# Self-attention stage: VectorE normalises the rows of the tile after next behind the second decay addition, and not at the beginning of the body

## The chip, the core and the metric

The kernel runs on one core of a Trainium2 chip. A core has five engines, each with an instruction queue of its own that is worked off in order: TensorE (PE in the profile, its weight loads PEld), VectorE (DVE), ScalarE (ACT), GpSimd (POOL) and SyncE (SP, which issues DMAs here). Engines meet only at semaphores: an instruction may wait until a semaphore has reached a value, and may raise one when it ends. An instruction that waits holds up everything behind it in its engine's queue. The metric is the device time of one launch in microseconds (us).

## What is computed

A layer with three parts, each adding to `x` (128 batches, 32 rows, width 128): a cross-attention over 257 context rows, a causal self-attention with a decay over the distance of rows, and a mixture of 8 experts. The change lies in the second part alone. Cut to what matters, that part is:

```python
Q, K, V = (proj(Wq, bq), proj(Wk, bk), proj(Wv, bv))        # of _layernorm(x); 16 heads of 8
scores = jnp.einsum('bhnd,bhmd->bhnm', Q, K) / jnp.sqrt(jnp.float32(dk))
scores = scores + power_law_mask(N, DECAY_SCALE)[None, None] # -0.25*log(lag), -inf above the diagonal
attn = jax.nn.softmax(scores, axis=-1)
out = jnp.einsum('bhnm,bhmd->bhnd', attn, V)
return out.transpose(0, 2, 1, 3).reshape(B, N, D) @ Wo + bo
```

## The kernel before

The three parts run one after the other, each in a block that all engines enter and leave together. The self-attention is the function `attend` (line 728 on). It works on 16 tiles of 8 batches. `X` holds the rows of all tiles in the core's memory, so this stage moves no data of its own from or to the chip's main memory.

The order of the work is written out by hand: every engine runs a function `body(t)` for t = 0 to 17, and each body has work of several tiles, so that the tiles run as a pipeline. What one tile goes through:

- VectorE takes statistics of the rows (`norm_stats`, `norm_mean`, `norm_var`, L791 to L803), GpSimd raises the variance to the power -1/2 (`power`, L910), and VectorE writes the normalised rows `xn` in two instructions (`norm`, L811).
- TensorE transposes `xn` (`turn`, L1005), ScalarE copies the result (`turned`, L941), TensorE projects it to queries and keys (`project`, L1011 and L1012), ScalarE spreads these (`projected`, L950 and L955).
- TensorE computes the scores in two halves of 4 batches (`scores`, L1033). For each half VectorE adds the decay (`add_decay`, L821), takes maxima (`maxima`, L826) and subtracts them (`less_maxima`, L831); ScalarE takes the exponential (L968); VectorE sums and inverts (L837, L842); GpSimd multiplies (`normalise`, L903, which writes `En`).
- TensorE transposes the probabilities (`turn_probs`, L1043), ScalarE copies them (`probs`, L975), TensorE multiplies them with the values (`weigh`, L1054), VectorE keeps each head's own part (`own`, L849), TensorE projects the output (`project_out`, L1064), GpSimd adds the output's bias to the rows (`bias`, L917), and VectorE adds the two (`add`, L857).

In body t the queues of the four engines hold, in this order:

- VectorE: `norm(t+2)`, then `add_decay(t,0)`, `maxima(t,0)`, `add_decay(t,1)`, `less_maxima(t,0)`, `maxima(t,1)`, `norm_stats(t+3)`, `less_maxima(t,1)`, `add(t-2)`, `norm_mean(t+3)`, the sums and inverses of both halves with `norm_var(t+3)` between, and `own(t-1)` for both halves.
- TensorE: `project(t+1)`, `scores(t,0)`, `scores(t,1)`, `turn_probs(t-1)` for both halves, `turn(t+2)`, `project_out(t-2)`, `values(t)`, `weigh(t-1)` for both halves.
- ScalarE: `projected(t+1)`, `probs(t-1,0)`, the exponential of half 0, `probs(t-1,1)`, the exponential of half 1, `turned(t+2)`, `values(t)`.
- GpSimd: `bias(t-2)`, `normalise(t,0)`, `power(t+3)`, `normalise(t,1)`.

So TensorE's `turn(t+2)` waits in body t for VectorE's `norm(t+2)` of the same body (L1001), and VectorE's `add_decay(t,h)` waits for TensorE's `scores(t,h)` (L817). `norm(t+2)` itself waits for `power(t+2)`, which GpSimd ran one body earlier, and for `turn(t+1)`, by which `xn` is free again.

Of the kernel before, what the change touches and what calls it, by code (L numbers as in the profile page):

```python
# [26 lines left out]
T = B // TB  # L27
# [700 lines left out]
def attend(nc, X, ident, hh_scaled, consts):  # L728


    with ExitStack() as s2:
# [42 lines left out]
        def tile_of(t):  # L774
            return X[:, t, :] if isinstance(t, int) else X[:, bass.ds(t, 1), :].rearrange("p a c -> p (a c)")

        def run(body):

            for t in range(T + 2):
                body(t)  # L780

        def later(t):
            return not (isinstance(t, int) and t == 0)

        with nc.Block() as block:
            @block.vector
            def _(dve):
                def norm_stats(t):
                    xt = tile_of(t)
                    for e in range(2):  # L790
                        i = dve.bn_stats(stat[:, e, :], xt[:, e * D:(e + 1) * D])  # L791
                    i.then_inc(n_stat, 1)

                def norm_mean(t):
                    dve.wait_ge(n_stat, t + 1)
                    dve.nop(nofuse=True)
                    for e in range(2):
                        i = dve.bn_aggr(mv[:, e, :], stat[:, e, :])
                    i.then_inc(n_mv, 1)

                def norm_var(t):
                    dve.wait_ge(n_mv, t + 1)
                    dve.tensor_scalar(var[:, :], mv[:, :, 1], EPS_LN, None, ALU.add).then_inc(n_var, 1)  # L803

                def norm(t):
                    dve.wait_ge(n_rs, t + 1)
                    if later(t):
                        dve.wait_ge(xt_ps, t)
                    xt = tile_of(t)
                    for e in range(2):  # L810
                        i = dve.tensor_scalar(xn[:, e, :], xt[:, e * D:(e + 1) * D], mv[:, e, 0:1], rs[:, e:e + 1],  # L811
                                              ALU.subtract, ALU.mult)
                    i.then_inc(n_xn, 1)

                def add_decay(t, h):
                    m = 2 * t + h
                    dve.wait_ge(s_ps, m + 1)  # L817
                    if later(t):
                        dve.wait_ge(en_sb, m - 1)
                    flat = E[:, h, :, :].rearrange("p u s -> p (u s)")  # L820
                    dve.tensor_tensor(flat, PS[h][:, :], decay[:, :, :].rearrange("p u s -> p (u s)"), ALU.add).then_inc(s_sb, 1)  # L821

                def maxima(t, h):
                    m = 2 * t + h
                    dve.wait_ge(s_sb, m + 1)
                    dve.tensor_reduce(mx[:, h, :], E[:, h, :, :], AX.X, ALU.max).then_inc(m_sb, 1)  # L826

                def less_maxima(t, h):
                    m = 2 * t + h
                    dve.wait_ge(m_sb, m + 1)  # L830
                    dve.tensor_tensor(E[:, h, :, :], E[:, h, :, :], mx[:, h, :].unsqueeze(2).to_broadcast([P, HB * NQ, L]),  # L831
                                      ALU.subtract).then_inc(d_sb, 1)

                def sums(t, h):
                    m = 2 * t + h
                    dve.wait_ge(e_sb, m + 1)
                    dve.tensor_reduce(sm[:, h, :], E[:, h, :, :], AX.X, ALU.add).then_inc(sum_sb, 1)  # L837

                def invert(t, h):
                    m = 2 * t + h  # L840
                    dve.wait_ge(sum_sb, m + 1)
                    dve.reciprocal(sm[:, h, :], sm[:, h, :]).then_inc(inv_sb, 1)  # L842

                def own(t, h):
                    m = 2 * t + h
                    dve.wait_ge(o_ps, m + 1)
                    if later(t):
                        dve.wait_ge(y_ps, t)
                    dve.tensor_tensor(Oc[:, :, HB * h:HB * h + HB, :].rearrange("p a b g -> p b a g"),  # L849
                                      PE_[h][:, :, :].rearrange("p j (a g) -> p j a g", g=NQ),  # L850
                                      hh_wide[:, :, :].rearrange("p q a -> p (q a)").unsqueeze(1).unsqueeze(3).to_broadcast(
                                          [P, HB, HQ * TB, NQ]), ALU.mult).then_inc(o_sb, 1)

                def add(t):
                    dve.wait_ge(y_ps, t + 1)
                    dve.wait_ge(xb, t + 1)
                    dve.tensor_tensor(tile_of(t), PY[:, :], Xb[:, :], ALU.add).then_inc(x2, 1)  # L857

                def body(t):
                    if t + 2 < T:  # L860
                        norm(t + 2)
                    if t < T:
                        add_decay(t, 0)
                        maxima(t, 0)
                        add_decay(t, 1)
                        less_maxima(t, 0)
                        maxima(t, 1)
                        if t + 3 < T:
                            norm_stats(t + 3)
                        less_maxima(t, 1)  # L870
                    if t >= 2:
                        add(t - 2)
                    if t + 3 < T:
                        norm_mean(t + 3)
                    if t < T:
                        sums(t, 0)
                        if t + 3 < T:
                            norm_var(t + 3)
                        invert(t, 0)
                        sums(t, 1)  # L880
                        invert(t, 1)
                    if 1 <= t <= T:
                        own(t - 1, 0)
                        own(t - 1, 1)

                for t in range(2):
                    norm_stats(t)
                    norm_mean(t)
                    norm_var(t)
                    norm(t)  # L890
                norm_stats(2)
                norm_mean(2)
                norm_var(2)
                run(body)

            @block.gpsimd
# [749 lines left out]
```

## Time and profile before

| | |
|---|---|
| median of 3 runs | 933.85 us (933.37 to 934.37) |
| the profiled execution | 933.31 us, of which its span (first to last instruction) is 931.4 us |
| span of the self-attention stage | about 459 to 620 us |
| busy in the span | PE 86%, DVE 87%, ACT 68%, POOL 44% |

Times in the trace are microseconds from the start of the span. A row of the timeline is a run of equal instructions: its start, the time from its first start to its last end, the engine, the line of the kernel, the operation, output<-inputs, the count, and in square brackets how long the engine sat idle before it and what released it. Instructions of one engine overlap a little, so what one costs in a busy queue is the time from its start to the next start.

### The profile page before, as it was taken

The page shows a single profiled execution, that of the slowest core. Times are in us where ns is not written, and L with a number is a line of the kernel's source. Part 1 is how long each engine was busy: PE and PEld are TensorE (multiplying, and loading weights), DVE is VectorE, ACT ScalarE, POOL GpSimd, SP SyncE. Part 2 cuts the span into 40 slices and gives each one's busy share as a digit, 9 for nine tenths or more (in the row PEclk, how much of TensorE's full clock was granted, in tenths as well). Part 3 has the DMA queues.
Part 4 walks back from the last instruction along what each step waited for, and adds up shares of the span by engine and source line. Part 5 has one row for each costly group of instructions (what it writes and reads, how often), then busy time and mean ns, then how long its engine had stood idle before and what let it go on. Part 6 is the DMA issues. An engine that isn't in the chain of part 4 may idle for free. (4 is left out here: it accounts for less than half of the span.)

```text
span 931.4 us, 32721 instructions
## 1 busy us (share of the span) xinstructions
PE 804.2 (86%) x10989; PEld 636.6 (68%) x10989; DVE 808.1 (87%) x2344; ACT 636.4 (68%) x2022; POOL 408.8 (44%) x420
## 2 busy tenths in 40 slices
PE   4898998899889889988669999979989898899882
PEld 2566666566666656665468888968878787788782
DVE  4888988988898889888659999957999999999994
ACT  3777777777777777777367777725767767776774
POOL 4222222322222222322114334344787777878785
PEclk9999999999999999999969999999999999999997
DMA  3221111111111111114000000000000000000000
GB/s 89 70 84 40 51 37 51 37 48 44 40 51 37 51 37 51 40 41 164 7 2 2 3 2 3 4 1 1 8 6 6 11 6 6 6 11 6 6 10 14
DMA packets 32717, 27.60 MB, mean 30 GB/s; under 512 B 3548, under 2 KB 32408, under 8 KB 32664
## 3 DMA queue, kind: packets, MB, share of 16 engines
q1 hardware_dynamic: 32664, 26.87, 9.8%
q8 instruction: 36, 0.59, 0.3%
q14 instruction: 17, 0.14, 0.1%
HBM read 24.76 MB, written 2.10 MB: 29 GB/s over the span
## 5 line engine op out<-in xcount | busy, mean ns | idle before, releaser
L544 ACT ACTIVATE E<-SC,neg_max 128x257 f32<-128x257 f32 x512 | 235.9, 474 | 101.8 <-DVE neg_max L604 101.8
L604 DVE TENSOR_REDUCE neg_max<-SC 128x1 f32<-128x257 f32 x512 | 181.9, 417 | 36.7 <-PE SC L401 34.1
L414 PE MATMUL ETP<-ident,E 128*128 128x128 f32 x1024 | 162.3, 286 | 37.9 <-ACT E L544 37.4
L613 DVE TENSOR_TENSOR Et<-ETP,mask_T 128x512 f32<-128x512 f32 x256 | 172.5, 684 | 15.5 <-PE ETP L414 14.4
L414 PEld LDWEIGHTS ETP<-ident,E 128*128 128x128 f32 x1024 | 108.8, 142 | 88.5 <-issue 78.4
L1311 PE MATMUL PO<-W,hid 128*128 128x128 f32 x1024 | 137.9, 278 | 18.7 <-ACT hid L1352 18.7
L1376 ACT ACTIVATE Y<-Z,zb,zs 128x128 f32<-128x128 f32 x256 | 111.0, 485 | 60.1 <-DVE zb L1531 60.1
L1311 PEld LDWEIGHTS PO<-W,hid 128*128 128x128 f32 x1024 | 131.2, 192 | 28.9 <-issue 21.5
L1300 PE MATMUL PH<-xT,W 128*128 128x256 f32 x512 | 135.4, 387 | 0.5 <-ACT xT L1344 0.5
L1352 ACT ACTIVATE hid<-PH,b1c 128x256 f32<-128x256 f32 x256 | 105.5, 463 | 19.3 <-PE PH L1300 17.8
L544 ACT ACTIVATION_READ_ACCUMULATOR E<-SC,neg_max 128x1 f32 x512 | 103.8, 203 | 0.0
L332 POOL TENSOR_TENSOR Qbd<-Qt,hh_scaled 128x512 f32<-128x512 f32 x32 | 40.7, 1272 | 131.1 <-ACT Qt L532 131.1
L401 PE MATMUL SC<-Kt,Qbd 32*128 32x257 f32 x1024 | 93.2, 433 | 2.1 <-DVE out_bias L709 0.6
L1300 PEld LDWEIGHTS PH<-xT,W 128*128 128x128 f32 x512 | 87.8, 192 | 9.7 <-ACT xT L1344 0.7
L433 PE MATMUL AV<-Et,V 128*32 128x128 f32 x2048 | 83.3, 279 | 0.1
L1202 POOL TENSOR_TENSOR XB<-xn,b2r 128x512 f32<-128x512 f32 x64 | 81.4, 1275 | 0.8 <-DVE xn L1427 0.8
L1208 POOL TENSOR_TENSOR zr<-zv,neg_half 128x8 f32<-128x8 f32 x32 | 60.0, 1875 | 39.6 <-DVE zv L1517 39.6
L1541 DVE TENSOR_TENSOR U<-Y,gr 128x512 f32<-128x512 f32 x64 | 71.2, 1112 | 5.4 <-POOL acc L1214 2.9
L903 POOL TENSOR_TENSOR En<-E,sm 128x512 f32<-128x512 f32 x32 | 33.4, 1048 | 95.4 <-DVE sm L842 95.4
L433 PEld LDWEIGHTS AV<-Et,V 128*32 128x32 f32 x2048 | 49.8, 109 | 32.6 <-DVE Et L613 26.3
L307 POOL TENSOR_TENSOR xrs<-xvar,neg_half 128x1 f32<-128x1 f32 x32 | 17.6, 550 | 119.3 <-DVE xvar L591 119.3
L525 ACT ACTIVATE Kt<-MISC 128x256 f32<-128x256 f32 x128 | 49.2, 384 | 25.5 <-PE MISC L382 17.4
(161 smaller groups left out, 1406.3 us busy)
## 6 DMA issues: line engine op xcount, KB each, us to landing
V<-in_ctx_dram SPq DMA_DIRECT2D x64, 256.0 KB, 2.6
xh<-in_x_dram SPq DMA_DIRECT2D x32, 64.0 KB, 2.2
last_rep<-in_ctx_dram SPq DMA_DIRECT2D x128, 2.0 KB
X<-in_x_dram SPq DMA_DIRECT2D x32, 64.0 KB
out_dram<-Xo SPq DMA_DIRECT2D x64, 32.0 KB, 1.5
W<-in_L_ffn_w_dram SPq DMA_DIRECT2D x1, 1024.0 KB
W<-in_L_ffn_w_dram SPq DMA_DIRECT2D x2, 512.0 KB
b2r<-in_L_ffn_b_dram SPq DMA_DIRECT2D x1, 512.0 KB
```

The source lines that it names most:

```text
L401: i = pe.matmul(SC[:, g, 0:S], Qbd[r, j // HB, j % HB, :, :].rearrange("p q l -> p (q l)"), Kt[r, j, :], start=True, stop=True)
L414: i = pe.transpose(ETP[s][:, c:c + P], E[:, j // HB, NQ * (j % HB) + 2 * s + u, k * P:(k + 1) * P], ident[:, :])
L433: i = pe.matmul(AV[32 * g:32 * g + 32, j % HB, :], V[:, j, k, 32 * g:32 * g + 32], Et[:, 2 * (j % 2) + g // 2, g % 2, k, :], start=(j % HB ...
L544: i = act.activation(E[:, h, at, :], SC[:, u, 0:S], ACT.Exp, bias=neg_max[:, j % 2, u:u + 1], accum_out=den[:, h, at:at + 1])
L604: dve.tensor_reduce(neg_max[:, j % 2, u:u + 1], SC[:, u, 0:S], AX.X, ALU.max, negate=True).then_inc(max_sb, 1)
L613: dve.tensor_tensor(Et[:, 2 * (j % 2) + s, :, :, :].rearrange("p u k c -> p (u k c)"), ETP[s][:, :], mask_T[:, :, :, :].rearrange("p u k c ...
L1202: pool.tensor_tensor(XB[:, 2 * p:2 * p + 2, :, :], xn[:, :, :].unsqueeze(1).to_broadcast([P, 2, 2, D]), b2r[:, 2 * p:2 * p + 2, :].unsquee ...
L1300: i = pe.matmul(PH[x % 2][:, a, :], W1[:, x, a * P:(a + 1) * P], xT[:, :], start=True, stop=True)
L1311: i = pe.matmul(PO[p % 2][:, 2 * (x % 2) + e, :], hid[:, x % 2, a, e * P:(e + 1) * P], W2[:, x, a, :], start=(a == 0), stop=(a == FH - 1))
L1352: i = act.activation(hid[:, x % 2, a, :], PH[x % 2][:, a, :], ACT.Gelu, bias=b1c[:, FH * x + a:FH * x + a + 1])
L1376: i = act.activation(Y[:, p % 2, k, :], Z[:, p, k, :], ACT.Identity, scale=zs[:, p // 2, f:f + 1], bias=zb[:, p // 2, f:f + 1])
L1541: dve.tensor_tensor(U[:, k, :, :].rearrange("p (x e) d -> p x e d", x=2), Y[:, k, :, :].rearrange("p (x e) d -> p x e d", x=2), gr[:, 2 * ...
```

## The change

In VectorE's `body(t)` the call of `norm(t + 2)` moves from the first place to the place behind `add_decay(t, 1)`. The functions that are called stay as they are, and so do the queues of the other engines.

```diff
                 def body(t):
-                    if t + 2 < T:
-                        norm(t + 2)
                     if t < T:
                         add_decay(t, 0)
                         maxima(t, 0)
                         add_decay(t, 1)
+                    if t + 2 < T:
+                        norm(t + 2)
+                    if t < T:
                         less_maxima(t, 0)
                         maxima(t, 1)
                         if t + 3 < T:
```

VectorE's queue where one body ends and the next begins, bodies 2 and 3, before (xn is the tile of normalised rows, PS the scores in the matmul output memory, E the scores with decay, Oc the heads' outputs; the names in brackets are the semaphores that an instruction waits for):

```order
L849 TENSOR_TENSOR Oc<-PE,hh_wide 128x4x32x4 [waits y_ps,o_ps2] x2
L811 TENSOR_SCALAR xn<-X,mv,rs 128x128 [waits xt_ps,n_rs]
L811 TENSOR_SCALAR xn<-X,mv,rs 128x128
L821 TENSOR_TENSOR E<-PS,decay 128x512 [waits en_sb,s_ps]
L826 TENSOR_REDUCE mx<-E 128x16 [waits s_sb]
L821 TENSOR_TENSOR E<-PS,decay 128x512 [waits en_sb,s_ps]
L831 TENSOR_TENSOR E<-E,mx 128x512 [waits m_sb]
```

and the same place now:

```order
L849 TENSOR_TENSOR Oc<-PE,hh_wide 128x4x32x4 [waits y_ps,o_ps2] x2
L821 TENSOR_TENSOR E<-PS,decay 128x512 [waits en_sb,s_ps]
L826 TENSOR_REDUCE mx<-E 128x16 [waits s_sb]
L821 TENSOR_TENSOR E<-PS,decay 128x512 [waits en_sb,s_ps]
L811 TENSOR_SCALAR xn<-X,mv,rs 128x128 [waits xt_ps,n_rs]
L811 TENSOR_SCALAR xn<-X,mv,rs 128x128
L831 TENSOR_TENSOR E<-E,mx 128x512 [waits m_sb]
```

The two instructions of `norm` stand behind two instructions that wait for the scores (`s_ps`); before, they stood ahead of them.

VectorE's queue at the end of the prologue and in body 0, before:

```order
L803 TENSOR_SCALAR var<-mv 128x2 [waits n_mv]
L811 TENSOR_SCALAR xn<-X,mv,rs 128x128 [waits xt_ps,n_rs]
L811 TENSOR_SCALAR xn<-X,mv,rs 128x128
L821 TENSOR_TENSOR E<-PS,decay 128x512 [waits s_ps]
L826 TENSOR_REDUCE mx<-E 128x16 [waits s_sb]
L821 TENSOR_TENSOR E<-PS,decay 128x512 [waits s_ps]
L831 TENSOR_TENSOR E<-E,mx 128x512 [waits m_sb]
```

and now:

```order
L803 TENSOR_SCALAR var<-mv 128x2 [waits n_mv]
L821 TENSOR_TENSOR E<-PS,decay 128x512 [waits s_ps]
L826 TENSOR_REDUCE mx<-E 128x16 [waits s_sb]
L821 TENSOR_TENSOR E<-PS,decay 128x512 [waits s_ps]
L811 TENSOR_SCALAR xn<-X,mv,rs 128x128 [waits xt_ps,n_rs]
L811 TENSOR_SCALAR xn<-X,mv,rs 128x128
L831 TENSOR_TENSOR E<-E,mx 128x512 [waits m_sb]
```

Here the normalisation of tile 2 leaves the prologue, in which VectorE waits for the first scores, and stands between instructions of body 0.

## Rows read from the trace of the kernel before

**Rows 1.** The page: busy time, share of the span, instructions of each engine.

```profile
PE 804.2 (86%) x10989; PEld 636.6 (68%) x10989; DVE 808.1 (87%) x2344; ACT 636.4 (68%) x2022; POOL 408.8 (44%) x420
```

**Rows 2.** Timeline of VectorE, one steady body (start, duration, engine, line, operation).

```profile
535.41 1.68 DVE L811 TENSOR_SCALAR xn<-X,mv,rs 128x128 f32<-128x128 f32 x2
537.01 0.68 DVE L821 TENSOR_TENSOR E<-PS,decay 128x512 f32<-128x512 f32 x1
537.73 0.69 DVE L826 TENSOR_REDUCE mx<-E 128x16 f32<-128x512 f32 x1
538.33 0.68 DVE L821 TENSOR_TENSOR E<-PS,decay 128x512 f32<-128x512 f32 x1
538.93 0.68 DVE L831 TENSOR_TENSOR E<-E,mx 128x512 f32<-128x512 f32 x1
...
544.43 1.68 DVE L811 TENSOR_SCALAR xn<-X,mv,rs 128x128 f32<-128x128 f32 x2
```

**Rows 3.** Timeline of GpSimd beside it.

```profile
535.28 1.05 POOL L903 TENSOR_TENSOR En<-E,sm 128x512 f32<-128x512 f32 x1
536.28 0.73 POOL L917 TENSOR_TENSOR Xb<-X,out_bias 128x256 f32<-128x256 f32 x1
```

**Rows 4.** Timeline of VectorE in the prologue.

```profile
461.31 0.60 DVE L811 TENSOR_SCALAR xn<-X,mv,rs 128x128 f32<-128x128 f32 x2 [0.82 <-POOL rs L910]
461.83 0.48 DVE L791 BATCH_NORM_STATS2 stat<-X 128x6 f32<-128x128 f32 x2
```

**Rows 5.** Timeline of TensorE, the same steady body.

```profile
533.22 0.70 PE L1011 MATMUL PA<-xT,Wq 128*128 128x256 f32 x2 [0.29 <-ACT xT L941]
...
534.19 1.95 PE L1033 MATMUL PS<-Kbd,Qbd 128*128 128x128 f32 x16
535.97 1.07 PE L1043 MATMUL PE<-ident,En 128*128 128x128 f32 x8
537.15 0.44 PE L1005 MATMUL PA<-ident,xn 128*128 128x128 f32 x2
537.42 1.95 PE L1064 MATMUL PY<-Wo,Oc 128*128 128x128 f32 x16
539.30 0.76 PE L1020 MATMUL PV<-Wv,xT 128*32 128x32 f32 x64
540.00 1.95 PE L1054 MATMUL PE<-Et,Vt 32*32 32x128 f32 x64
```

**Rows 6.** Timeline of TensorE, first half of the scores of the next body.

```profile
543.21 1.05 PE L1033 MATMUL PS<-Kbd,Qbd 128*128 128x128 f32 x8
```

**Rows 7.** Timeline of TensorE in the last bodies.

```profile
591.26 0.44 PE L1005 MATMUL PA<-ident,xn 128*128 128x128 f32 x2
...
597.06 1.95 PE L1033 MATMUL PS<-Kbd,Qbd 128*128 128x128 f32 x16
...
602.29 1.95 PE L1054 MATMUL PE<-Et,Vt 32*32 32x128 f32 x64
604.17 2.05 PE L1033 MATMUL PS<-Kbd,Qbd 128*128 128x128 f32 x16
```

**Rows 8.** Timeline of TensorE in bodies 1 and 2.

```profile
479.03 1.22 PE L1011 MATMUL PA<-xT,Wq 128*128 128x256 f32 x2 [3.18 <-ACT xT L941]
...
488.47 0.70 PE L1011 MATMUL PA<-xT,Wq 128*128 128x256 f32 x2
...
492.09 0.40 PE L1005 MATMUL PA<-ident,xn 128*128 128x128 f32 x2
```

**Rows 9.** Timeline of VectorE in body 1.

```profile
484.55 0.69 DVE L821 TENSOR_TENSOR E<-PS,decay 128x512 f32<-128x512 f32 x1 [0.30 <-PE PS L1033]
...
486.74 0.67 DVE L831 TENSOR_TENSOR E<-E,mx 128x512 f32<-128x512 f32 x1
```

**Rows 10.** Windows: length, busy us per engine, then PEclk, DMA share, GB/s.

```profile
476.00:479.00 3.00, 0.00 (x0) 0.00 (x0) 3.00 (x11) 1.73 (x5) 0.07 (x1) 0.86 0.02 5
488.00:590.00 102.00, 97.87 (x1954) 88.53 (x1943) 101.03 (x228) 74.84 (x173) 39.84 (x47) 1.00 0.01 3
611.00:619.00 8.00, 6.57 (x117) 5.70 (x107) 3.25 (x7) 1.20 (x2) 3.05 (x4) 1.00 0.01 2
```

## The prediction

> **What bounds the kernel now.** I read the page first: over the whole span no engine stands out, PE and DVE are at 86% and 87% [rows 1]. That is a mean over three stages, so next come the windows of the stage that the change touches. In the 102 us of its steady bodies VectorE is busy 101.03 us, TensorE 97.87 us [rows 10]: VectorE has no gap left and sets the pace. The timeline gives the pace: `norm` starts at 535.41 and again at 544.43, a body every 9.02 us [rows 2].
>
> Then I ask what each instruction of that full queue costs, and one is odd. The two instructions of `norm` hold VectorE from 535.41 to 537.01, 1.60 us [rows 2]. In the prologue the same two hold it from 461.31 to 461.83, 0.52 us, and end 0.60 us after they start [rows 4]. What differs is GpSimd: in the steady body `En` runs from 535.28 to 536.33 and `Xb` from 536.28 to 537.01 [rows 3], so `norm` runs beside GpSimd from end to end; its last instruction ends at 537.09, 0.08 us behind `Xb`. In the prologue GpSimd is idle meanwhile. So about 1.08 us of each body is time that `norm` loses beside GpSimd.
>
> The last view is TensorE's. It is almost as full, and in its queue `turn` stands in the middle: it starts at 537.15, 0.06 us behind the end of `norm`, while `turn_probs` ahead of it ended at 535.97 + 1.07 = 537.04 [rows 5]. So TensorE waits for `norm` even now, by some 0.1 us of empty array, and behind `turn` stand the longest pieces of the body. This wait decides the change.
>
> **The change part by part.** It adds and removes no instruction and no DMA. It moves two VectorE instructions past three others, in 14 bodies.
>
> *What VectorE saves.* GpSimd's `En` and `Xb` follow VectorE's inverses of the same body, and end 1.60 us behind the last `own` (535.41 to 537.01 [rows 2, 3]). In the new place `norm` comes 1.92 us behind `own` (add 0.72, maxima 0.60, add 0.60 [rows 2]), and later still by any wait for the scores. It then runs with GpSimd idle. I take 0.52 us of queue as in the prologue; the bounds are 0.52 and 1.60. VectorE's own work falls from 9.02 to 7.94 us a body. Were VectorE alone the limit, that would be 1.08 us a body.
>
> *What TensorE loses.* `norm(t+2)` now waits behind both halves of `scores(t)`, and TensorE's `turn(t+2)` of the same body waits for it. Behind `turn` in the queue stand `project_out`, `values` and `weigh`, then the next body's `project` and `scores`, and for those the next `add_decay` waits. That closes a ring through both engines which did not exist before: scores, add, maxima, add, norm, turn, and on to the next scores. Its length, piece by piece:
>
> - `turn` to `project_out` 0.27, to `values` 1.88, to `weigh` 0.70 [rows 5]. `weigh` to what follows: 1.88 where the next matmuls are ready (602.29 to 604.17 [rows 7]). Together 4.73.
> - `project` to `scores`: 534.19 - 533.22 = 0.97 [rows 5]. The 0.29 us that `project` waits for ScalarE now falls away, since ScalarE's copy hangs on the second `less_maxima`: from that to `project` it takes 1.73 (486.74 to 488.47 [rows 8, 9]), and in the ring more than 3 us lie between them.
> - First half of the scores to `add_decay(t,0)`: 1.05 for its matmuls [rows 6] and 0.05 for the crossing to VectorE, an estimate from the 0.06 of norm to turn above. 1.10.
> - `add_decay` 0.72, `maxima` 0.60, the second `add_decay` 0.60 [rows 2]. The second half of the scores (1.95 from the start of the 16 matmuls [rows 5]) is there in time: the second addition starts 1.10 + 1.32 = 2.42 behind that start.
> - `norm` 0.60 to its end [rows 4], 0.06 to `turn`.
>
> Sum: 4.73 + 0.97 + 1.10 + 1.92 + 0.60 + 0.06 = 9.38 us. VectorE's 7.94 lies inside and gains idle time instead of pace. The body goes from 9.02 to 9.38 us, 0.36 longer. On TensorE the same is seen as a pause: from the start of the scores to `turn` 3.68 us (before 537.15 - 534.19 = 2.96), of which scores and `turn_probs` fill 1.78 + 1.07, so 0.83 us stays empty. The bounds: with `weigh` at its whole duration, 1.95, the body takes 9.45; if matmuls, crossing and `norm` each overlap the next by a few hundredths more than I let them, 9.25. I take 9.38, made of start-to-start times throughout.
>
> *The start.* In body 0 `norm(2)` leaves a time in which VectorE was idle and enters its busy chain: `less_maxima` and all behind it, the exponentials and ScalarE's copy for `project(2)`, come 0.52 later, so `project(2)` moves from 479.03 [rows 8] to 479.55, and with it the scores and the second addition of body 1, from 484.55 [rows 9] to 485.07. `less_maxima(1,1)` follows 2.19 + 0.52 later (486.74 - 484.55 = 2.19 [rows 9]) at 487.78, 1.04 late; `project(3)`, which hangs on it, moves from 488.47 to 489.51. From there to `turn(4)` it is 0.97 + 3.68 = 4.65, so 494.16 against 492.09 [rows 8]: 2.07 late.
>
> *The steady part.* From `turn(4)` to `turn(15)` before: 591.26 - 492.09 = 99.17 in 11 bodies [rows 7, 8], 9.02 each. Now 11 x 9.38 = 103.18, 4.0 more.
>
> *The end.* From `turn(15)` to the scores of body 14 it was 597.06 - 591.26 = 5.80 [rows 7], now 4.73 + 0.97 = 5.70: 0.1 back. Bodies 14 to 17 have no `norm`, and TensorE runs through them without pause at first, so nothing else is given back. The expert stage begins after all engines have met and is unchanged.
>
> Sum: 2.07 + 4.0 - 0.1 = 6.0 us. On the profiled execution's own time, 933.31 (span 931.4 and 1.9 around it), that is 939.3; on the median of the runs, 0.54 higher, it is 939.85. I forecast 939.5.
>
> *The clock.* A longer pause in every body could cost TensorE its clock. In 476 to 479 it had no matmul and its granted clock fell (mean 0.86); the project of 479.03 took 1.22 us against 0.70 at full clock [rows 5, 8, 10]. In 611 to 619 it stood empty for 1.43 of 8 us, a larger share than 0.83 of 9.38, and kept 1.00, the level of 2.4 GHz [rows 10]. So I put the clock at no cost. The Trainium skill, "TensorE: Matmul & The Clock Gate", section "A second HAM failure mode: psum-queue depth-cycling", speaks against this: it tells of a kernel in which small pauses between groups of matmuls in every iteration made the clock swing and cost throughput. By that rule the change would end as the fourth rival below; the steady bodies of before, with their small pauses at 1.00, do not show it.
>
> **The rivals.**
>
> *1. Faster: VectorE was the limit, and its 1.08 us come through.* The place is `add_decay(t,0)`, which can start earlier once `norm` is gone from ahead of it; it decides if the stretch from scores to `turn` comes in under 2.96 + 0.36 = 3.32 us, so that the ring is no longer than 9.02. The floor is then TensorE's own work, 97.87 / 102 x 9.02 = 8.65 us a body [rows 10]; 12 bodies at 0.37 less, 4.4 us, give 929.5. For it speaks VectorE's full queue. Against it: three VectorE instructions of 0.60 or more and `norm` itself lie one behind the other in that stretch, and none of them can start before the scores.
>
> *2. No change.* The saved VectorE time and TensorE's wait pay for one another: the ring is some 0.3 shorter than the sum of its pieces and the start costs less, because more of it lies beside waits for the first scores. Then the body stays at 9.0 and the time at 933 to 935.5. Against it: every piece is a start-to-start time already, with the overlap in it.
>
> *3. It does not do what it says: `norm` meets GpSimd in the new place too.* Then the ring is 1.08 longer, 10.46 us, and 12 bodies add 13 us: 952. Against it: `Xb` ended 1.60 us behind `own`, and the new `norm` starts behind `own` by 1.92 us of other instructions and by VectorE's new idle time, 9.38 - 7.94 = 1.44, or 3.36 in all.
>
> *4. The clock falls in the pause.* At 1.22 against 0.70 us for the same matmuls the 6.8 us of TensorE in the ring become some 11.8, 5 us more in each body that it strikes; in every fifth body 11 us more, 950.
>
> **How the numbers follow.** Two runs of this kernel differ by up to 1 us, so under 0.2% (1.9 us) is no change. Forecast 0.76, rival 1 0.07, rival 2 0.09, rival 3 0.03, rival 4 0.05. Slower: forecast and rivals 3 and 4, 0.84; same 0.09; faster 0.07. The forecast's own range: body 9.25 to 9.45 (2.5 to 4.7 us), start 1 to 2.5, so 3.5 to 7 us more, 936.8 to 940.9. The range of 8 in 10 reaches down into the no-change case, 935, and up by the unknown price of `norm` behind a busy queue, 942.
>
> **What would show it.** Right: `norm` at some 0.6 us for its two instructions in the steady bodies; VectorE idle before `add_decay(t,0)` for about 1.2 us, released by TensorE's scores; TensorE's `turn` waiting for `xn` for about 0.8 us in each of 12 bodies; the wait of `project` for ScalarE gone; a body of 9.38 us, VectorE under 90% busy in it. Wrong: a body under 9.02 us, with `turn` free of waits (rival 1); `norm` still above 1.2 us (rival 3); a granted clock under 1.00 between 490 and 600 (rival 4).

## The result and the profile after

The changed kernel is slower: 940.8 us median (939.32 to 940.96) against 933.93 (933.37 to 934.37), four runs each, ratio 1.007, 95% interval 1.0053 to 1.0088. A second set of runs of the same two kernels, on one chip, gave 939.95 against 932.24, ratio 1.007 (1.0049 to 1.0091). The forecast was 939.5, its range 935 to 942. The profiled execution has a span of 937.4 us, 6.0 more than before.

The page after, busy time and share of the span, against [rows 1]:

```profile
PE 801.3 (85%) x10989; PEld 634.8 (68%) x10989; DVE 796.9 (85%) x2344; ACT 637.3 (68%) x2022; POOL 409.3 (44%) x420
```

VectorE works 11.2 us less than before and the kernel takes longer: the work saved has turned into waiting. Where it waits, the timeline of VectorE in a steady body shows, against [rows 2] (start, duration, what ran, in brackets the idle time ahead and what ended it):

```profile
535.82 1.22 DVE L849 TENSOR_TENSOR Oc<-PE,hh_wide 128x512 f32<-128x512 f32 x2
538.16 0.69 DVE L821 TENSOR_TENSOR E<-PS,decay 128x512 f32<-128x512 f32 x1 [1.12 <-PE PS L1034]
538.89 0.69 DVE L826 TENSOR_REDUCE mx<-E 128x16 f32<-128x512 f32 x1
539.49 0.68 DVE L821 TENSOR_TENSOR E<-PS,decay 128x512 f32<-128x512 f32 x1
540.09 0.60 DVE L811 TENSOR_SCALAR xn<-X,mv,rs 128x128 f32<-128x128 f32 x2
...
547.53 0.69 DVE L821 TENSOR_TENSOR E<-PS,decay 128x512 f32<-128x512 f32 x1 [1.12 <-PE PS L1034]
```

`norm` takes 0.60 us for its two instructions and not 1.68. In exchange VectorE stands idle for 1.12 us ahead of the first decay addition, until TensorE has the scores. The body takes 547.53 - 538.16 = 9.37 us; before it was 9.02.

The timeline of TensorE in the same body, against [rows 5]:

```profile
536.10 0.70 PE L1012 MATMUL PA<-xT,Wq 128*128 128x256 f32 x2
...
537.07 1.95 PE L1034 MATMUL PS<-Kbd,Qbd 128*128 128x128 f32 x16
538.86 1.04 PE L1044 MATMUL PE<-ident,En 128*128 128x128 f32 x8
540.74 0.44 PE L1006 MATMUL PA<-ident,xn 128*128 128x128 f32 x2 [0.85 <-DVE xn L811]
541.02 1.95 PE L1065 MATMUL PY<-Wo,Oc 128*128 128x128 f32 x16
542.90 0.76 PE L1021 MATMUL PV<-Wv,xT 128*32 128x32 f32 x64
543.59 1.95 PE L1055 MATMUL PE<-Et,Vt 32*32 32x128 f32 x64
545.47 0.70 PE L1012 MATMUL PA<-xT,Wq 128*128 128x256 f32 x2
```

`turn` (L1006) waits 0.85 us for `norm`; the 0.29 us ahead of `project` are gone. The ring can be walked here: scores at 537.07, first addition at 538.16 (1.09 later), second at 539.49, `norm` 540.09 to 540.69, `turn` at 540.74, `project` at 545.47 (4.73 later), next scores 0.97 behind that. GpSimd's timeline, against [rows 3], shows that it is out of the way: its bias ends at 538.58, 1.5 us before `norm` starts.

```profile
536.83 1.05 POOL L904 TENSOR_TENSOR En<-E,sm 128x512 f32<-128x512 f32 x1
537.84 0.74 POOL L918 TENSOR_TENSOR Xb<-X,out_bias 128x256 f32<-128x256 f32 x1
```

The waits of 488 to 600 us (who waited for whom: total us, times, longest) and the window of the steady bodies, against [rows 10], say the same for all of them:

```profile
PEld PA L1006 <- DVE xn L811: 13.0, 12, 1.1
DVE E L821 <- PE PS L1034: 12.1, 11, 1.3
PE PA L1006 <- DVE xn L811: 10.2, 12, 0.8
```

```profile
488.00:596.00 108.00, 98.51 (x1984) 90.26 (x1973) 93.15 (x232) 76.20 (x174) 40.98 (x48) 1.00 0.01 3
```

VectorE is busy 93.15 of 108 us, 86%, where it had been 99%; TensorE 91%, where it had been 96%. The granted clock is 1.00 throughout.

**Where the 6.0 us are.** The stage begins with VectorE's first statistics and ends with those of the expert stage; `turn(4)` and `turn(15)` divide it. "Again" is the profile of the second set of runs.

| stretch | before | after | more | again | more | forecast |
|---|---|---|---|---|---|---|
| ahead of the stage | 459.45 | 460.63 | 1.18 | 460.10 | 0.65 | 0 |
| start, to `turn(4)` | 32.64 | 33.29 | 0.65 | 34.77 | 2.13 | 2.07 |
| `turn(4)` to `turn(15)` | 99.17 | 103.35 | 4.18 | 103.02 | 3.85 | 4.0 |
| to the expert stage | 29.41 | 29.30 | -0.11 | 29.31 | -0.10 | -0.1 |
| expert stage | 310.73 | 310.83 | 0.10 | 312.00 | 1.27 | 0 |
| span | 931.4 | 937.4 | 6.0 | 939.2 | 7.8 | 6.0 |

The steady bodies and the end agree with the forecast in both profiles. The start does so in the second alone; that the first profile's whole span comes out at the forecast 6.0 is luck, since the 1.4 us missing at its start are made up by 1.18 ahead of the stage, 0.18 in the steady bodies and 0.10 in the expert stage. In the first, TensorE's clock rose earlier, while the first scores were still being computed. The first scores, `project(2)`, `project(3)` and `turn(4)` in the first profile, against [rows 8]:

```profile
472.58 2.52 PE L1034 MATMUL PS<-Kbd,Qbd 128*128 128x128 f32 x16
...
480.13 0.81 PE L1012 MATMUL PA<-xT,Wq 128*128 128x256 f32 x2 [2.18 <-ACT xT L942]
...
489.28 0.70 PE L1012 MATMUL PA<-xT,Wq 128*128 128x256 f32 x2 [0.16 <-ACT xT L942]
...
493.92 0.44 PE L1006 MATMUL PA<-ident,xn 128*128 128x128 f32 x2 [0.85 <-DVE xn L811]
```

and in the second:

```profile
472.05 3.62 PE L1034 MATMUL PS<-Kbd,Qbd 128*128 128x128 f32 x16
...
480.27 1.22 PE L1012 MATMUL PA<-xT,Wq 128*128 128x256 f32 x2 [2.18 <-ACT xT L942]
...
490.23 0.70 PE L1012 MATMUL PA<-xT,Wq 128*128 128x256 f32 x2 [0.16 <-ACT xT L942]
...
494.87 0.44 PE L1006 MATMUL PA<-ident,xn 128*128 128x128 f32 x2 [0.85 <-DVE xn L811]
```

The granted clock (the first of the last three numbers) while the first scores are computed, in the first profile:

```profile
474.00:475.00 1.00, 1.00 (x10) 0.90 (x9) 0.72 (x2) 1.00 (x3) 0.00 (x0) 1.00 0.00 0
```

and in the second:

```profile
473.00:475.00 2.00, 2.00 (x11) 2.00 (x11) 0.97 (x2) 1.99 (x5) 0.00 (x0) 0.50 0.00 0
```

From the beginning of the stage to `project(2)` it is 19.50 us in the first profile and 20.17 in the second, from `project(2)` to `project(3)` 9.15 and 9.96. The differences ahead of the stage and in the expert stage are not put down to the change: in the twelve profiles of this study the stage began between 459.35 and 463.29 us, though nothing ahead of it differs, and two kernels below that hold the change began it at 459.35 and 459.68, about where the kernel before did. Of the 1.27 us in the second profile's expert stage 1.20 arise ahead of VectorE's first addition into `Z` (L1486), which comes 11.49 us behind that stage's beginning and not 10.29, at a mean granted clock of 0.70 and not 0.83.

### The profile page after: what moved, and what is told of

Its sections match the earlier page's. It is cut to its first block and busy times, and to the rows that moved or that the text cites. A ratio compares the mean times of both kernels' runs of the same rounds, so it can differ in the third digit from the quotient of the medians.

```text
span 937.4 us, 32721 instructions
## 1 busy us (share of the span) xinstructions
PE 801.3 (85%) x10989; PEld 634.8 (68%) x10989; DVE 796.9 (85%) x2344; ACT 637.3 (68%) x2022; POOL 409.3 (44%) x420
```

## The experiments

The theory is the ring: scores, add, maxima, add, `norm`, `turn`, `project_out`, `values`, `weigh`, `project`, scores. Its rivals: the start or the new place as such costs the time; or VectorE's load alone counts. Each edit is against the changed kernel unless said. "Body" is the time from one `turn` to the next in the steady part of the profile.

**The changed kernel again**, for its size.

> The changed kernel unchanged, beside the kernel before on one chip, to measure the size on more runs. Ring theory: a body of 9.37 us against 9.02, and a start that costs 0.7 to 2.1 us according to when TensorE's clock rises: 4.6 to 6.0 us more than the kernel before. Rival (the part of the first profiled pair that lay ahead of the stage, 1.2 us, belongs to the change): 6 to 7.2 us more.

Measured: 939.95 against 932.24, 7.7 more by the medians, 4.6 to 8.5 by the interval. The median lies above both what the theory and what the rival expected, and the interval holds both, so the total does not decide between them. The profile does: the stage has 5.9 of the 7.8 us, inside the 4.6 to 6.0 of the theory, and the rest lies in stretches that the change does not touch. What makes those differ from one execution to the next stays open, but for the granted clock at the beginning of the expert stage.

**`norm` behind the first maxima.**

```diff
                         maxima(t, 0)
-                        add_decay(t, 1)
                     if t + 2 < T:
                         norm(t + 2)
                     if t < T:
+                        add_decay(t, 1)
                         less_maxima(t, 0)
```

> norm stands behind the first maxima, one VectorE instruction (0.60 us) earlier than in the changed kernel. Ring theory: the ring of both engines is 9.38 - 0.60 = 8.78 us, so a body takes 8.8 us, under the 9.02 of the kernel before, and 11 to 12 bodies save 2.6 to 2.9 us, of which the start may take up to 2 back: 931 to 934 us. TensorE still waits for norm, some 0.25 us a body; norm stays at 0.60 us, because GpSimd's bias ends before it starts. Rival (the slowdown is a cost of the start or of taking norm out of the head of the body, not of the ring): as slow as the changed kernel, 939 to 941 us.

Measured: 932.77 against 934.17, ratio 0.9984 (0.9973 to 0.9995). TensorE's `turn` in two bodies:

```profile
538.64 0.44 PE L1006 MATMUL PA<-ident,xn 128*128 128x128 f32 x2 [0.25 <-DVE xn L811]
547.40 0.44 PE L1006 MATMUL PA<-ident,xn 128*128 128x128 f32 x2 [0.25 <-DVE xn L811]
```

8.76 us a body and a wait of 0.25, 0.60 less of both than in the changed kernel. One VectorE instruction of 0.60 us decides between slower than before and no slower. By the medians this kernel is 1.4 us faster than the one before; the interval does not reach a ratio of 1, but the prediction calls anything under 1.9 us no change.

**`norm` behind the first addition.**

```diff
                         add_decay(t, 0)
-                        maxima(t, 0)
-                        add_decay(t, 1)
                     if t + 2 < T:
                         norm(t + 2)
                     if t < T:
+                        maxima(t, 0)
+                        add_decay(t, 1)
                         less_maxima(t, 0)
```

> norm stands behind the first decay addition, 1.2 us earlier than in the changed kernel. Ring theory: without GpSimd the ring would be 8.1 us and TensorE's own work, some 8.35 us a body, would set the pace; but norm now starts some 0.8 us behind own, when GpSimd's bias (to 1.6 us behind own) still runs, so norm is stretched to 0.9 to 1.3 us and the body takes 8.35 to 8.6 us: 5 to 8 us less than the kernel before, 926 to 930 us. Rival (VectorE's load alone counts): 7.94 + 0.5 us a body, the same as e1 or faster by little; rival (the head of the body matters): 939 to 941 us.

Measured: 930.42 against 934.17, ratio 0.9958 (0.9944 to 0.9971), 0.4 us slower than the range expected. From `turn(4)` at 493.43 to `turn(15)` at 587.48 it is 94.05 us, 8.55 a body. `norm` pays for GpSimd's company again, as VectorE's and GpSimd's timelines show:

```profile
543.58 1.10 DVE L811 TENSOR_SCALAR xn<-X,mv,rs 128x128 f32<-128x128 f32 x2
```

```profile
542.61 1.05 POOL L904 TENSOR_TENSOR En<-E,sm 128x512 f32<-128x512 f32 x1
543.61 0.72 POOL L918 TENSOR_TENSOR Xb<-X,out_bias 128x256 f32<-128x256 f32 x1
```

TensorE still waits for it, in the weight load of `turn`:

```profile
544.73 0.20 PEld L1006 LDWEIGHTS PA<-ident,xn 128*128 128x128 f32 x2 [0.27 <-DVE xn L811]
```

**TensorE's `turn` later, `norm` as in the change.** Two versions; the first:

```diff
-                    if t + 2 < T:
-                        turn(t + 2)
                     if t >= 2:
                         project_out(t - 2)
                     if t < T:
                         values(t)
+                    if t + 2 < T:
+                        turn(t + 2)
```

> The changed kernel with one further edit: on TensorE turn(t+2) stands behind project_out and values and not ahead of them, so that norm has 2.6 us more until it is waited for. Ring theory: the ring is cut, TensorE never waits for norm, VectorE's 7.94 us and TensorE's own work, 8.35 us, set the pace: 8.35 to 8.5 us a body, 0.5 to 0.67 us less than the kernel before in 11 to 12 bodies, 925 to 929 us. Rival (norm in this place is slow for VectorE or the start costs it): no faster than 937 us, since VectorE's queue is the same as in the changed kernel.

Measured: 929.08 against 934.17, ratio 0.9945 (0.9931 to 0.9959), at the upper end of what was expected; `turn` without a wait:

```profile
540.02 0.44 PE L1006 MATMUL PA<-ident,xn 128*128 128x128 f32 x2
548.47 0.44 PE L1006 MATMUL PA<-ident,xn 128*128 128x128 f32 x2
```

8.45 us a body with VectorE's queue exactly that of the change. The place of `norm` is slow only through who waits for it. The second version puts `turn` between `project_out` and `values`:

```diff
-                    if t + 2 < T:
-                        turn(t + 2)
                     if t >= 2:
                         project_out(t - 2)
+                    if t + 2 < T:
+                        turn(t + 2)
                     if t < T:
                         values(t)
```

> The changed kernel with turn(t+2) on TensorE directly behind project_out and ahead of values: norm has 1.88 us more until it is waited for, which is more than the pause of 0.85. Ring theory: no wait for norm, 8.3 to 8.45 us a body, 4 to 6 us less than the kernel before, as e3 or up to 2 us faster. Rival (turn must stand behind values, or ScalarE's copy comes too late): slower than e3.

Measured: 925.49 against 932.24, ratio 0.9918 (0.9898 to 0.9938): faster than both kernels, and the fastest of the study. `turn` in two bodies, 8.30 us apart, and the window of the steady bodies, in which the profile shows TensorE busy throughout:

```profile
536.70 0.38 PE L1006 MATMUL PA<-ident,xn 128*128 128x128 f32 x2
...
545.00 0.38 PE L1006 MATMUL PA<-ident,xn 128*128 128x128 f32 x2
```

```profile
490.00:590.00 100.00, 100.00 (x2091) 93.83 (x2091) 95.98 (x238) 79.17 (x181) 41.95 (x50) 1.00 0.01 3
```

**The same TensorE edit on the kernel before**, `norm` at the head of the body.

```diff
-                    if t + 2 < T:
-                        turn(t + 2)
                     if t >= 2:
                         project_out(t - 2)
                     if t < T:
                         values(t)
+                    if t + 2 < T:
+                        turn(t + 2)
```

> The kernel before, norm at the head of the body, with the same TensorE edit as e3. Ring theory: VectorE's full queue, with 1.60 us of norm beside GpSimd, sets 9.02 us a body, so freeing TensorE of its wait changes nothing: 933 to 935 us, VectorE without idle time, norm still 1.68 us. Rival (TensorE's order alone gives the gain of e3): as fast as e3, 925 to 929 us.

Measured: 933.21 against 934.17, ratio 0.999 (0.9982 to 0.9999), and `norm`, 9.02 us apart:

```profile
538.99 1.69 DVE L811 TENSOR_SCALAR xn<-X,mv,rs 128x128 f32<-128x128 f32 x2
...
548.01 1.69 DVE L811 TENSOR_SCALAR xn<-X,mv,rs 128x128 f32<-128x128 f32 x2
```

So before the change VectorE's queue with its 1.60 us of `norm` was the limit. Neither edit alone gains as both do: `turn` behind `values` gives 9.02 us a body here and 8.45 together with the change.

**One more VectorE instruction ahead of `norm`, or behind it.** The line with (1) or the one with (2):

```diff
                         add_decay(t, 1)
+                        dve.tensor_reduce(spare[:, :], decay[:, :, :], AX.X, ALU.max)   # (1)
                     if t + 2 < T:
                         norm(t + 2)
                     if t < T:
+                        dve.tensor_reduce(spare[:, :], decay[:, :, :], AX.X, ALU.max)   # (2)
                         less_maxima(t, 0)
```

> The changed kernel with one more maximum (of the decay table, 512 elements, into a spare tile that nobody reads) on VectorE ahead of norm, 14 to 16 times. Ring theory: the new instruction lies in the ring, so each body grows by its 0.60 us although VectorE has 1.1 us to spare: 9.97 us a body, 7 to 8.5 us more than the changed kernel, 946 to 949 us; TensorE waits 1.45 us for norm and not 0.85. Rival (VectorE's load counts, and it has room): no more than the changed kernel, 939 to 941 us.

> The same extra instruction, but behind norm and not ahead of it. Ring theory: it lies outside the ring and takes its 0.60 us out of VectorE's idle 1.1 us ahead of the first decay addition: a body stays at 9.37 us, the idle time falls to 0.5, and only the start and the last bodies, where VectorE has no idle time, can cost some 0.6 to 2 us: 940 to 943 us. Rival (any VectorE work in the body costs its time): 946 to 949 us, as e5.

Measured: ahead 950.01 against 932.14, ratio 1.018 (1.0164 to 1.0195); behind 942.28, ratio 1.0105 (1.009 to 1.0119). `turn` with the extra instruction ahead:

```profile
535.56 0.44 PE L1008 MATMUL PA<-ident,xn 128*128 128x128 f32 x2 [1.44 <-DVE xn L812]
545.52 0.44 PE L1008 MATMUL PA<-ident,xn 128*128 128x128 f32 x2 [1.44 <-DVE xn L812]
```

and with it behind:

```profile
532.68 0.44 PE L1008 MATMUL PA<-ident,xn 128*128 128x128 f32 x2 [0.85 <-DVE xn L812]
542.04 0.44 PE L1008 MATMUL PA<-ident,xn 128*128 128x128 f32 x2 [0.85 <-DVE xn L812]
```

9.96 against 9.36 us a body for the same work. Ahead of `norm` its 0.60 us come in full, though VectorE idles more than a microsecond in every body; behind it they come out of idle time. The idle time ahead of the first addition falls to 0.75 us, as VectorE's timeline shows, and not to the expected 0.5:

```profile
539.47 0.69 DVE L822 TENSOR_TENSOR E<-PS,decay 128x512 f32<-128x512 f32 x1 [0.75 <-PE PS L1036]
```

The other 0.22 come out of a shorter wait ahead of `add`, which starts 0.81 us behind the second `less_maxima` in the changed kernel (542.19 to 543.00) and 0.59 behind it here (534.72 to 535.31). The first median lies 1 us above what was expected, the second inside; the two differ by 7.7 us, some 13 bodies of 0.60.

**GpSimd's work beside `norm` taken away**, in the kernel before.

```diff
-                    pool.tensor_tensor(En[:, h, :, :], E[:, h, :, :], sm[:, h, :].unsqueeze(2).to_broadcast([P, HB * NQ, L]),
+                    u = HB * NQ if h == 0 or t == 0 else 1
+                    pool.tensor_tensor(En[:, h, 0:u, :], E[:, h, 0:u, :], sm[:, h, 0:u].unsqueeze(2).to_broadcast([P, u, L]),
                                        ALU.mult).then_inc(en_sb, 1)
...
+                    c = D if t == 0 else 1     # and the bias over the first c columns of each half alone
```

> The kernel before, norm at the head of the body, but GpSimd's second En of a tile and its bias are cut to a few elements from tile 1 on (this leaves work out: half the probabilities and most of the rows with bias stay those of tile 0). Theory of GpSimd's company: with nothing long on GpSimd beside it norm takes 0.6 us and not 1.68, VectorE's body 7.95 us, and TensorE's own work sets the pace at 8.35 to 8.5: 925 to 929 us. Rival (norm is slow at the head of the body for another reason, its place behind own or a wait): norm stays above 1.4 us and the time at 932 to 935 us.

Measured: 926.23 against 932.14, ratio 0.9934 (0.9922 to 0.9945). VectorE at the head of the body:

```profile
538.35 0.59 DVE L811 TENSOR_SCALAR xn<-X,mv,rs 128x128 f32<-128x128 f32 x2
539.23 0.69 DVE L821 TENSOR_TENSOR E<-PS,decay 128x512 f32<-128x512 f32 x1 [0.28 <-PE PS L1035]
```

The same two instructions in the old place take 0.59 us once GpSimd is nearly idle beside them, and the body takes 8.30. The shorter work on GpSimd can help TensorE in other ways too; what `norm` costs is read from its own row.

**GpSimd's company given back to `norm`**, in the changed kernel.

```diff
                     if 2 <= t:
                         bias(t - 2)
+                    if 2 <= t < T:
+                        pool.wait_ge(s_sb, 2 * t + 2)
+                        flat = decay[:, :, :].rearrange("p u s -> p (u s)")
+                        pool.tensor_tensor(spare[:, :], flat, flat, ALU.mult)
```

> The changed kernel with one more GpSimd multiplication (512 elements of the decay table by themselves, into a spare tile that nobody reads) that starts when the second decay addition has ended, so beside norm, in bodies 2 to 15. Theory of GpSimd's company: norm is held until that instruction ends, 1.2 to 1.3 us and not 0.6, and as norm lies in the ring each body grows by 0.6 to 0.7: 946 to 949 us. Rival (GpSimd's company costs norm nothing): norm stays at 0.60 us and the time at 939 to 941.

Measured: 948.9 against 932.14, ratio 1.0182 (1.0169 to 1.0195). VectorE's two instructions of `norm`, one by one, and GpSimd's beside them:

```profile
543.07 0.34 DVE L812 TENSOR_SCALAR xn<-X,mv,rs 128x128 f32<-128x128 f32 x1
543.32 1.06 DVE L812 TENSOR_SCALAR xn<-X,mv,rs 128x128 f32<-128x128 f32 x1
```

```profile
543.23 1.07 POOL L928 TENSOR_TENSOR spare<-decay 128x512 f32<-128x512 f32 x1 [1.68 <-DVE E L822]
```

The first started alone and takes 0.34; the second starts 0.09 us after GpSimd's instruction and ends 0.08 behind it, after 1.06. Together they take 1.31, where 1.2 to 1.3 was expected. With the ring longer by that, `turn` waits 1.57 us and the body takes 10.09.

## Why the prediction was right

- *What VectorE saves.* Forecast 1.08 us a body, with `norm` at 0.52 us of its queue. Measured 0.51 (540.09 to 540.60), VectorE busy 86% of the steady bodies. That GpSimd's company had cost the difference was argued from two stretches of one trace; taking it away and giving it back shows it.
- *What TensorE loses.* Forecast ring 9.38 us, measured 9.37; pause of `turn` 0.83 and 0.85; VectorE's wait for the scores 1.2 and 1.12, where another line of the working had 1.44 for all of VectorE's idle time (0.22 more lie ahead of `add`). Not every piece is a start-to-start time, as the working says: the first half of the scores (1.05) and `norm` (0.60) go in by their durations, each with a crossing to the next engine, the one to VectorE as an estimate. They came out as forecast, 1.09 for 1.10 and 0.65 for 0.66. That the ring, and not VectorE's load, sets the time is shown by the extra instruction that costs 0.60 ahead of `norm` and nothing in the steady bodies behind it, and by `turn` moved later, which removes the loss with VectorE's order unchanged.
- *The start.* Forecast 2.07, measured 2.13 and 0.65. The working took the clock's rise from the trace of before as given; in the first profile it came earlier and gave back 1.4 us. That the second agrees to 0.06 rests on a rise that came about as late as before (first scores of 3.62 us, 3.54 before).
- *The rivals.* Rival 1 (VectorE's 1.08 us come through) fell: the stretch from scores to `turn` is 3.67 us (537.07 to 540.74), above the 3.32 below which it would hold. Rival 2 (no change) fell with it: the ring is not some 0.3 shorter than the sum of its pieces, but 0.01. `norm` one instruction earlier has a stretch under 3.32 and a body under 9.02, as rival 1's condition says. Rival 1's floor of 8.65 us was too high: it counted TensorE's busy time before as work that can't shrink, and two experiments run at 8.30. Against that floor the changed kernel loses 1.07 us a body, which is about what the weight load of `turn` waits for `norm` (13.0 us in 12 bodies); the gap between the matmuls shows 0.85 of it. Rival 3 fell with `norm` at 0.60 us; its price, 1.08 a body with both instructions held, was 0.72 in the experiment that held one. Rival 4 fell: the clock stayed at 1.00 with pauses of 0.85, and also, from 490 to 600 us, with 1.44 and 1.57 in the two slowest experiments. The Trainium skill, "TensorE: Matmul & The Clock Gate", section "A second HAM failure mode: psum-queue depth-cycling", tells of a kernel whose small pauses between groups of matmuls made the clock swing; the steady bodies here do not show it.
- *The size.* The medians differ by 6.9 and 7.7 us, the sum said 6.0. The stage itself accounts for 4.7 and 5.9 in the two profiles; the rest lies outside it and changes from execution to execution. The prediction took 1 us for the spread of two runs of one kernel, from three runs; 23 runs of the kernel before lie between 932.02 and 936.93.

## What to carry to other kernels

An instruction that a second engine waits for in the middle of its queue is placed by that wait, not by where its own engine is cheapest: walk the ring through both queues and add its start-to-start times. Moving it behind something that the second engine produces closes a ring; then move the waiting instruction back as well, and both gains come together (8.45 us a body here with `turn` behind `values`, where that move alone gave 9.02 and the move of `norm` alone 9.37; 8.30 with `turn` behind `project_out`, a move that was not run alone). An engine that loses work and gains idle time, at a longer body, is how such a ring looked here.

## What the runs showed of the hardware

A VectorE instruction of 0.34 us, one that scales and shifts rows in the core's memory, is held here when a GpSimd instruction is under way as it starts: it takes 1.06 us beside one of 1.07 that started 0.09 us before it, and ends 0.08 us behind it, not its own 0.34. An instruction that started 0.16 us before GpSimd's takes its 0.34. In the steady body of the kernel before, both instructions of `norm` end 0.08 us behind a GpSimd instruction, `En` and `Xb`. With `norm` behind the first addition the first of its two starts while `En` has 0.08 us left and 0.03 us before `Xb` starts, and is held until `Xb` too has ended:

```profile
543.58 0.84 DVE L811 TENSOR_SCALAR xn<-X,mv,rs 128x128 f32<-128x128 f32 x1
```

Why it was not let in between the two is open. GpSimd's instructions are not slowed: `En` takes 1.05 us and `Xb` 0.73 beside `norm` [rows 3], 1.05 and 0.74 without it in the changed kernel.

The Trainium skill, "SBUF — State Buffer", section "SBUF: two separate sides", has the two engines share a pair of ports that one holds for a whole instruction while the other blocks, where VectorE's instruction is in a mode that uses two ports or reads two inputs from this memory beside a GpSimd instruction that reads it; which mode `norm` runs in no trace here shows. The direction agrees, but an instruction that was blocked to the end and then ran in full would have ended some 0.26 us later than it did (0.34 - 0.08).
